# Routing sixteen token tiles in batches of twelve and four instead of eight and eight

## The reference, cut to what matters

```python
x = x + linear_attention(adaptive_attention(x, cond))      # x1 below
h = x @ wt.T ; g = cond @ wg.T                             # router: 8 experts
scores = softmax((h + g) / 2) ; w, idx = top_k(scores, 2)
y = sum_r w[r] * expert[idx[r]](x)                         # leaky(x Wg) * (x Wu) @ Wd
y = y + shared_experts(x)                                  # two shared ones of the same form
x = x + relu(y @ W1 + b1) @ W2 + b2
```

## Time and profile before

| | us |
|---|---|
| median of 3 runs | 546.78 |
| the three runs | 546.78, 544.27, 547.57 |
| span of the profiled execution (first to last instruction) | 532.0 |
| median less span (what lies around the span) | 14.8 |

### The profile page before, as it was taken

One profiled execution on the slowest core, in us unless ns is written; L12 is line 12 of the kernel. 1 busy time (PEld: TensorE's weight loads), 2 busy tenths in 40 slices (PEclk: granted clock), 3 DMA queues, 4 the chain that ended last, 5 costly groups with the idle time before them and its releaser, 6 DMA issues.

```text
span 532.0 us, 11898 instructions
## 1 busy us (share of the span) xinstructions
PE 468.7 (88%) x3961; PEld 418.7 (79%) x3961; DVE 359.7 (68%) x879; ACT 274.7 (52%) x574; POOL 284.7 (54%) x343
## 2 busy tenths in 40 slices
PE   3946889999999999999999896499989489999997
PEld 1735777898999988898888785398989359898986
DVE  4784888888889888898766475757664524444522
ACT  3426666576667666566652422246565234453442
POOL 3738778897987979797830777400000633425100
PEclk9966999999999999999998998989999879999999
DMA  8370103709082641000010323265752312213011
GB/s 263 90 192 1 31 1 111 257 26 343 0 292 72 208 157 30 0 30 1 1 31 2 99 100 108 82 206 185 235 169 100 89 33 57 80 41 96 25 41 39
DMA packets 51616, 52.17 MB, mean 98 GB/s; under 512 B 6645, under 2 KB 49015, under 8 KB 51577
## 3 DMA queue, kind: packets, MB, share of 16 engines
q1 hardware_dynamic: 47956, 42.98, 25.5%
q0 software_dynamic: 3072, 8.39, 5.0%
q10 hardware_dynamic: 548, 0.28, 0.2%
HBM read 22.03 MB, written 29.62 MB: 97 GB/s over the span
## 4 chain that ended last, share of the span: by engine, by line
PE 59%; issue 8%; POOL 8%; ACT 5%; DMA 3%; DVE 3%; SPq 1%; DVEq 0%; ACTq 0%; POOLq 0%
PE bank L317 10%; PE bank L318 9%; PE bank L319 9%; POOL slot_x L579 6%; PE bank L322 5%; PE bank L323 5%; PE bank L1375 3%; PE bank L1655 3%; PE bank L1400 2%; PE bank L1339 2%; PE bank L1443 2%; ACT qT L666 2%; PE bank L1351 1%; PE bank L1388 1%; DMA slot_y<-yb 1%
## 5 line engine op out<-in xcount | busy, mean ns | idle before, releaser
L588 POOL DMA_INDIRECT yg<-slot_y,yrow x32 | 34.2, 1068 | 120.8 <-DMA slot_y<-yb 76.3
L561 POOL TENSOR_TENSOR rn<-sc,half 128x6 f32<-128x6 f32 (+1 forms) x48 | 60.6, 1277 | 7.9 <-DVE sc L1023 6.9
L1256 DVE TENSOR_TENSOR hl<-hw,hh 128x512 fp32r<-128x512 f32 x32 | 22.2, 693 | 57.1 <-ACT hw L837 57.1
L835 ACT ACTIVATE hh<-bank,late 128x512 fp32r<-128x512 f32 x32 | 22.0, 688 | 53.5 <-PE bank L1655 41.9
L317 PE MATMUL bank<-wqkv_h,xnT_h 128*128 128x384 f32 x96 | 39.1, 408 | 6.8 <-DVE sim L1004 6.8
L556 POOL TENSOR_TENSOR sim<-sim,mx 128x1040 f32<-128x1040 f32 x16 | 31.3, 1955 | 23.0 <-DVE mx L1007 23.0
L695 ACT ACTIVATE sq<-bank 128x384 f32<-128x384 f32 (+1 forms) x48 | 22.8, 475 | 40.3 <-PE bank L319 24.7
L524 POOL TENSOR_TENSOR biasm<-bias,mneg 128x1040 f32<-128x1040 f32 x16 | 35.7, 2229 | 3.7 <-DMA bias<-rel_scratch 3.7
L579 POOL DMA_INDIRECT slot_x<-xs,posi x32 | 31.4, 980 | 11.2 <-issue 9.4
L542 POOL TENSOR_TENSOR pr<-pe,rden 128x1024 f32<-128x1024 f32 x16 | 30.4, 1903 | 9.2 <-DVE rden L1044 4.5
L322 PE MATMUL bank<-wout_h,oT_h 128*128 128x256 f32 x128 | 33.6, 296 | 1.9 <-DVE oT_l L1038 1.9
(11 more groups left out here) (317 smaller groups left out, 1604.8 us busy)
## 6 DMA issues: line engine op xcount, KB each, us to landing
slot_x<-zrow SPq DMA_DIRECT2D x4, 4352.0 KB, 14.4
xq<-slot_x SPq DMA_DIRECT2D x40, 128.0 KB, 2.1
slot_y<-yb SPq DMA_DIRECT2D x20, 256.0 KB, 2.4
fstage<-in_f_W SPq DMA_DIRECT2D x4, 512.0 KB, 4.5
out<-p_all SPq DMA_DIRECT2D x8, 256.0 KB, 2.1
xs<-in_x SPq DMA_DIRECT2D x1, 1536.0 KB, 9.5
raw_out<-in_c_Wout SPq DMA_DIRECT2D x1, 1024.0 KB, 7.8
stage<-in_m_wgate SPq DMA_DIRECT2D x8, 128.0 KB, 2.1
```

The costliest lines, as they stand in the source:

```text
L561: e.tensor_tensor(rn[:, lo:hi], sc[:, lo:hi], half[:, lo:hi], ALU.pow).then_inc(sems['rn'], 1)
L588: e.indirect_dma_start(out=yg[:, g % 2, r, t, :], out_offset=None, in_=ydram.ap()[:, :], in_offset=bass.IndirectOffsetOnAxis(ap=yrow[:, g ...
```

## The change

The batches become twelve tiles (groups 0, 1, 2) and four tiles (group 3).

- PE: `x_transpose(1)` and `logits(0)` run behind the body of step 15, `x_transpose(2)` and `logits(1)` inside step 16, `logits(2)` behind the body of step 16. `x_transpose(2)` is gone from step 17, and `logits(2)` from behind the pipeline.
- ACT and DVE: the copies of group 0 move into step 15, those of group 1 behind step 15, those of group 2 into step 16, those of group 3 ahead of `unit_gate(0)` and `unit_leak(0)`.
- The routing functions stay where they are and take their batch's size: `router_logits(0)`, `router_top(0)` and `router_places(0)` for twelve tiles, those of batch 1 for four.
- POOL: the same 32 scatters in the same order; the first 24 wait for `pos` of batch 0, the last 8 for that of batch 1.
- Memory: `sq` and `qn` move to right behind the projection weights, `x1C` (group 2) overlays the end of the projection weights, `sq` and `qn`, and `x1D` (group 3) takes `x1B`'s place.

```diff
-BATCHES = ((0, 8), (8, 8))
+BATCHES = ((0, 12), (12, 4))
...
+        x1C_h = sb('x1C_h', [P, KD, GT], F32R)
+        x1C_l = sb('x1C_l', [P, KD, GT], F32R)
...
-        x1B_h = sb('x1B_h', [P, KD, 2 * GT], F32R)
-        x1B_l = sb('x1B_l', [P, KD, 2 * GT], F32R)
+        x1D_h = sb('x1D_h', [P, KD, GT], F32R)
+        x1D_l = sb('x1D_l', [P, KD, GT], F32R)
...
 # ACT
-            before_squares = {-1: before_first_squares, 0: wvo_upper, NT: lambda: x_upper(1)}
+            before_squares = {-1: before_first_squares, 0: wvo_upper, NT - 1: lambda: first_x(), NT: lambda: x_upper(2)}
-            pipeline(e, body, {-1: wout_upper, 0: decay_exp, 1: decay_log, 2: lambda: [decay_power(), wt_upper()], NT - 1: first_x, NT: lambda: router_exp(0), NT + 1: lambda: x_upper(2)})
+            pipeline(e, body, {-1: wout_upper, 0: decay_exp, 1: decay_log, 2: lambda: [decay_power(), wt_upper()], NT - 1: lambda: x_upper(1), NT: lambda: router_exp(0)})
+            x_upper(3)
             unit_gate(0)
-            x_upper(3)
...
 # DVE
-            before_sums = {..., 3: wt_lower, NT: lambda: x_lower(1), NT + 1: lambda: router_places(0)}
-            before_lower = {LAST_I: lambda: x_lower(2)}
+            before_sums = {..., 3: wt_lower, NT - 1: lambda: x_lower(0), NT: lambda: x_lower(2), NT + 1: lambda: router_places(0)}
-            pipeline(e, body, {-2: after_first_stats, NT - 1: lambda: x_lower(0), NT: after_values})
+            pipeline(e, body, {-2: after_first_stats, NT - 1: lambda: x_lower(1), NT: after_values})
+            x_lower(3)
             unit_leak(0)
-            x_lower(3)
...
 # PE
-            def third_x():
-                ranks(0)
-                x_transpose(2)
-            while_retrieving = {NT: lambda: x_transpose(1), NT + 1: third_x, LAST_I: first_gate}
-            before_values = {NT - 1: first_x, NT: lambda: logits(0)}
-            pipeline(e, body, {..., NT: lambda: logits(1)})
+            while_retrieving = {NT: lambda: x_transpose(2), NT + 1: lambda: ranks(0), LAST_I: first_gate}
+            before_values = {NT - 1: first_x, NT: lambda: logits(1)}
+
+            def second_x():
+                x_transpose(1)
+                logits(0)
+            pipeline(e, body, {..., NT - 1: second_x, NT: lambda: logits(2)})
             e.wait_ge(sems['x1'], due(NT))
             x_transpose(3)
-            logits(2)
             up(0)
             logits(3)
```

More of the change, by code:

```diff
@@ L95, in adaln_attention_ffn @@
             wqkv_l = s1('wqkv_l', [P, KD, QKV], F32R)
+            sq = s1('sq', [P, H + 1, DH])
+            qn = s1('qn', [P, H, DH])
             stage = s1('stage', [P, 3 * D])
@@ L182, in adaln_attention_ffn @@
         le = sb('le', [P, NT, E])
+        gap = sb('gap', [P, 64])
         unit_stage = sb('unit_stage', [P, 3 * D])
-        x1B_h = sb('x1B_h', [P, KD, 2 * GT], F32R)
-        x1B_l = sb('x1B_l', [P, KD, 2 * GT], F32R)
+        x1D_h = sb('x1D_h', [P, KD, GT], F32R)
+        x1D_l = sb('x1D_l', [P, KD, GT], F32R)
         w1_h = sb('w1_h', [P, KD, INTER], F32R)
@@ L300, in x_parts @@
         def x_parts(g, k):
-            h, l = (x1A_h, x1A_l) if g < 2 else (x1B_h, x1B_l)
-            at_g = slice(g % 2 * GT, (g % 2 + 1) * GT)
-            return (h[:, k, at_g], l[:, k, at_g])
+            if g >= 2:
+                h, l = (x1C_h, x1C_l) if g == 2 else (x1D_h, x1D_l)
+                return (h[:, k, :], l[:, k, :])
+            at_g = slice(g * GT, (g + 1) * GT)
+            return (x1A_h[:, k, at_g], x1A_l[:, k, at_g])
         def gate_bank(n):
@@ L572, in body, with scatter @@
                     mask_bias(i + 1)
+            def scatter(t0, t1):
+                for t in range(t0, t1):
+                    for r in range(2):
+                        e.indirect_dma_start(out=xdram.ap()[:, :], out_offset=bass.IndirectOffsetOnAxis(ap=posi[:, t, r:r + 1], axis=0), in_=xs[:, t, :], in_offset=None).then_inc(sems['st_x'], 16)
             pipeline(e, body, {-2: after_norm0, -1: after_first_projection, 0: after_first_scores, 1: after_second_scores, 2: mask_decay})
@@ L576, in _ @@
                 e.wait_ge(sems['pos'], due(b + 1))
-                for t in range(t0, t0 + n):
-                    for r in range(2):
-                        e.indirect_dma_start(out=xdram.ap()[:, :], out_offset=bass.IndirectOffsetOnAxis(ap=posi[:, t, r:r + 1], axis=0), in_=xs[:, t, :], in_offset=None).then_inc(sems['st_x'], 16)
+                scatter(t0, t0 + n)
             split_unit(U - 1)
@@ L968, in wt_lower @@
                 e.wait_ge(sems['v_lower'], upto('v_lower'))
-            before_sums = {-1: before_first_sums, 0: wvo_lower, 1: decay_sum, 2: decay_rate, 3: wt_lower, NT: lambda: x_lower(1), NT + 1: lambda: router_places(0)}
-            before_lower = {LAST_I: lambda: x_lower(2)}
+            before_sums = {-1: before_first_sums, 0: wvo_lower, 1: decay_sum, 2: decay_rate, 3: wt_lower, NT - 1: lambda: x_lower(0), NT: lambda: x_lower(2), NT + 1: lambda: router_places(0)}
             before_norms = {-1: fold_qk}
@@ L1520, in first_gate @@
                 gate(0)
-            while_retrieving = {NT: lambda: x_transpose(1), NT + 1: third_x, LAST_I: first_gate}
-            before_values = {NT - 1: first_x, NT: lambda: logits(0)}
-            pipeline(e, body, {-1: after_first_projection, 0: after_first_scores, 1: after_second_scores, NT: lambda: logits(1)})
+            while_retrieving = {NT: lambda: x_transpose(2), NT + 1: lambda: ranks(0), LAST_I: first_gate}
[3 more added lines that the diff above has]
+                logits(0)
+            pipeline(e, body, {-1: after_first_projection, 0: after_first_scores, 1: after_second_scores, NT - 1: second_x, NT: lambda: logits(2)})
             e.wait_ge(sems['x1'], due(NT))
             x_transpose(3)
-            logits(2)
             up(0)
```

3 lines of the change are left out of this document (removed).

## The result

| | us |
|---|---|
| the kernel before, median of 4 runs (lowest to highest) | 547.17 (544.27 to 548.3) |
| the kernel after, median of 4 runs (lowest to highest) | 554.5 (550.5 to 555.79) |
| ratio, 95% interval | 1.0135 (1.0091 to 1.0179) |
| profiled execution of after: time, span | 555.79, 554.0 |

The change makes the kernel slower, by 7.3 us here, and the forecast (551.3, up to 554.4) is 3.2 us too low. One line of the table already takes a step of the prediction away: in every execution that is listed with its span, of any kernel in this text, the time is the span and 1.7 to 1.95 us. So nothing like 14.8 us lies around a span. The profiled execution of before, with its span of 532.0, was one of about 534 us, and the runs it was set beside took 547. It was not an execution of the kind that was timed.

A forecast was written before the change was run, and what follows sets the result against it. First posi plus 32 scatters at 1.265 us pitch were taken to bound the kernel; 3.05 (PE) + 1.23 (routing) + 0.17 (places) = 4.45 us later, on 546.8 gives 551.3 us, range 545.8 to 554.4.

The forecast's parts named there:

- PE thus has 4.7 us of slack at this place, and the scatters have none: Ahead of the expert phase: PE idles 4.69 us for xq until all scatters land, so the scatters set the end.
- 3.05 + 1.23 + 0.17: Delay of the first posi: PE's added work, routing for twelve tiles, router_places(0); sum 4.45 us for all that follows.
- The span and the 14.8 us around it are the median of the runs: Base of the forecast: profiled span 532.0 us plus 14.8 around it taken as the median, 546.78.
- The second batch's positions come in time: At the seventeenth scatter: the second batch's posi is there 1.0 us before POOL comes to it, so no wait.
- Item 6: POOL: 24 scatters behind the first wait, start 4.45 us later at 300.6; second batch's positions by 318, needed at 331.
- The rival that the second batch did hold up POOL: Between sixteenth and seventeenth scatter: with a pitch below 1.22 us POOL waits there; at 0.96, 0.6 us gained, 546.2; chance 0.10.
- Items 1, 3 and 4: Ahead of the first posi: PE's added transposes and logits 3.05 us, routing chain for twelve tiles 1.23, router_places(0) 0.17.
- nothing that a later start would be hidden in: From the expert phase on: PE, gather and dense layer follow each other, so a later start is paid in full.
- The clock rival: PE's clock falls 3 to 6 us earlier, onto step 16's path; price 1.5 us, time 552.8; chance 0.20.
- the row at 266: Evidence against the clock rival: at 266 to 268 PE did almost only transposes and 8-column matmuls, yet clock stayed 1.00.
- Item 7: PE behind the pipeline: starts 4.45 us later, 2.17 less work, ends shared experts about 341, before xq at 348; slack grows.

The follow-up runs named there:

- 546 chip: The one chip, met by r1, r2, r3, r7 and r8, where the kernel before took 546.1 and 546.5 us.
- r1: The kernel before, unchanged, run and profiled again on the 546 chip: 545.74 us, ratio 1.0004.
- r2: The kernel after, unchanged, run and profiled again on the 546 chip: 550.25 us, ratio 1.0064.
- 532 chips: The three other chips, where the kernel before took 531.8, 534.1, and 532.6 and 532.3 us.
- r10: The kernel before with only one of each token's two scatters in the first batch, on one of the 532 chips: 532.95 us, ratio 0.9965.
- r16: The kernel before with each scatter moving half of each row, same kernel as r12, on another of the 532 chips: 534.29 us, ratio 1.0018.
- r12: The kernel before with each scatter moving half of each row, on one of the 532 chips; profiled execution 541.52 us.
- r3: The kernel after with batches put back to eight and eight tiles, the moved transposes and logits kept, on the 546 chip: 547.0 us, ratio 1.0036.
- r13: The kernel after, unchanged, on one of the 532 chips: 538.97 us to before's 534.08, ratio 1.0092.
- r7: The kernel after, unchanged, a third time, on the 546 chip: 550.22 us, ratio 1.006.
- r11: The kernel before with a pause of 16 chained memsets on POOL behind every eighth scatter, on one of the 532 chips: 541.3 us, ratio 1.0099.
- r8: The kernel before with all scatters held until the second batch's posi, on the 546 chip: 558.93 us, ratio 1.025.
- r4: The kernel before with all scatters held until the second batch's posi, same kernel as r8, on one of the 532 chips: 552.76 us.

## Why the prediction was right or wrong

**The step that failed.** "PE thus has 4.7 us of slack at this place, and the scatters have none": this was read from an execution of the other kind. In the traces of the 546 chip and of the first set's after, nobody waits for the last scatter. PE's expert phase starts on `p_all`, when PE's own work behind the pipeline is done, at 355.75 in r1 and 361.37 in r2, while `xq` is asked for at 350.86 in r2. So the sum 3.05 + 1.23 + 0.17 was made on a chain that is not the path there. The term that it put at nothing is the clock ahead of the first batch's `lg`, which cost 1.3 us in r2 and 2.9 in the profile of after. How much of the median each of the two is worth stays open, since no execution of before was profiled in the first set's runs.

**The base, wrong.** "The span and the 14.8 us around it are the median of the runs": 1.8 us lie around a span. The step took two kinds of execution for one. I had 546.78 beside 532.0 and explained the gap by something that no row showed.

**"The second batch's positions come in time", right where before takes 532, wrong where it was timed.** On 532 chips at full clock it holds (r10: `posi` at 314.79; r16: an unbroken chain). It fails when the clock falls behind the pipeline (r12: 5.26 us) and in every profile of the 546 chip with two batches of eight and scatters that aren't held (r1: 10.36 us; r3: 10.49). Item 6's "the wait is gone as a danger, but it wasn't there" has the danger right: after the change the wait is none in r13, 5.13 us in r2, 6.13 in the profile of after. The rival that the second batch did hold up POOL was right as to the place, but its mechanism (a smaller pitch) and its result were not: the pitch is 1.265 us in all runs.

**Items 1, 3 and 4, right where the clock stays up.** In r13, with a clock of 1.00 from 275 to 279 and 0.98 from 284 to 290, the moved transposes and logits take 3.13 us (271.37 to 274.50; worked out 3.05), `lg` to `bn_stats` 6.45 (6.4), `bn_stats` to `posi` 4.50 (4.49). The first scatter is at 300.92 for 300.6, PE's start 4.8 us later than in the earlier trace rows for 4.45, and the median 4.9 us. As a ratio, 1.0092 for the 1.008 forecast. That the medians agree so well is in part luck. Before's median of 534.08 has 8 slower executions in it; its 17 at a clock of 0.955 or more have 532.9, and all ten of after, at 0.946 to 0.952, lie 2.9 to 8.7 us above that. The two profiled spans differ by 3.5 us, so "nothing that a later start would be hidden in" is not right to the last us either.

**The clock rival, right in its mechanism on the 546 chip.** From the output projection's start to `lg` it was 14.43 us in the earlier trace rows and 14.35 in r13. In r2, with a clock of 0.60 from 275 to 279, it was 15.74 (274.45 to 290.19), and in the profile of after, where it was 0.58 there and 0.72 from 284 to 290 as well, ahead of `lg`, it was 17.32 (r2 has 1.00 in this second stretch, r13 0.98). r7, with 0.58 and 0.72, has 17.37. That is 1.3 and 2.9 us ahead of the first `posi`, for 1.5 in the rival. I gave it 0.20 because of the row at 266. The Trainium skill (TensorE: Matmul & The Clock Gate, PE-mode transpose) speaks for such a fall, as I had noted; r2 and after have it behind the same instructions, and r13 does not (its clock from 275 to 279 is 1.00), so that rule by itself doesn't tell when it comes.

**Item 7, wrong on both kinds.** "Slack grows": in r13 PE's wait for `xq` is 2.25 us and not over 4.69. PE ends the shared experts' work at 346.05, 7.2 us later than before and not at 341. Most of that is the pipeline's end: the transposes of the last group start 6.5 us later, not 4.45, with a clock of 0.64 from 290 to 304 where before has 1.00. The first line is of before, the second of r13:

```profile
300.84 1.09 PE L1450 MATMUL bank<-ident,xs 128*128 128x128 f32 x8 [0.52 <-DVE xs L1047]
307.30 1.10 PE L1456 MATMUL bank<-ident,xs 128*128 128x128 f32 x8 [0.52 <-DVE xs L1053]
```

On the 546 chip there was never slack here: PE's own work, stalled beside the scatters, sets the start (r1, r2, r3, after). There PE's start moves by what the change delays PE's own work, not by what it delays the last scatter (5.6 and 2.1 us from r1 to r2).

**The size.** Three sets of after against before give 1.0135, 1.0064 and 1.006 at 546 us, and one 1.0092 at 534. The forecast of 1.008 lies between them; on the 546 chip that is luck, since another path sets the time there. The first set's 554.5 is 0.1 over the range; its four runs have a mean clock of 0.935 to 0.947, towards the lower end of what r2's ten show (0.935 to 0.953, 555 to 546 us). That the clock goes with the time is in every list of runs; what makes it lower in one execution than in the next is not settled. Nor is it tested whether the first set's chip is of one kind with that of r1.

## What to carry to other kernels

Set the profiled execution's span beside the times before building on it: if they differ by more than the 2 us seen elsewhere, the profile shows another kind of execution, and a slack or a wait of it may not exist in those that are timed. Of a chain that waits for another engine in two places, ask for each place what the clock or a stall there would do: here a batch of twelve shields the last scatters from a slow PE, but makes all scatters start 5 to 7 us later (r13, r2), and where PE's own work ends last the shield gains nothing. Work put ahead of the first signal of a long serial chain is paid nearly in full where that chain ends last (r11: 7.4 us of chain, 7.3 of time; r13: 4.8 and 3.5 between two spans).

## What the runs showed of the hardware

- The same kernel took 542.1 to 548.5 us in 39 runs on one chip and 530.7 to 541.5 in 62 runs on three others. The difference is made around the scatters: PE's expert phase starts at 355.75 in r1 and at 343.54 in the earlier trace rows, and the spans are 540.5 and 532.0.
- On the 546 chip the other engines stall beside a run of indirect DMAs (32 of 128 rows of 1 KB at 1.265 us each): 9.13 us on DVE in r1, 28.42 on PE in r8, where POOL's own pitch stays 1.265. The first instruction that comes late starts 13.0 us behind the first scatter in r1 (DVE at 308.16, 2.4 us behind the execution shown, whose DVE is 0.9 us behind r1's up to there; scatters from 295.19) and 17.1 us in r8 (ACT at 332.86, 330.70 in r4; scatters from 315.73). On the 532 chips the same instructions show nothing of it. The cause is open; the DMA view shows no load of instructions at the end of either stall.
- PE's clock at half speed for 14 us behind the pipeline (0.55 from 306 to 320 in r12) was there in one of two profiled executions of one kernel and not in the other (r16: 1.00). They are of two chips, but on each of these the kernel took both about 532.6 us, at a mean clock of 0.961, and about 541.6, at 0.943. Of the 9 us between the two (541.52 to 532.58) 5.3 are the wait of a serial chain on POOL for an instruction late in PE's queue.
